# The hydra blocks' way in and way out: tokens halved by GpSimd and turned by DMAs, epsilon on GpSimd, orders listed anew

## What is computed

```python
x = L0_attn_hidden_states                                        # (4, 512, 512)
x = _layernorm(x + _L0_attn_ref(x, Wq, Wk, Wv, Wo), axis=-1)     # 32 heads of 16, causal, grouped keys
x = _layernorm(x + _L0_ffn_ref(x, gate, up, down), axis=-1)      # 4 bit weights, inner width 1376
x = _layernorm(x + _L1_attn_ref(x, ...), axis=-1)                # the hydra part
x = _layernorm(x + _L1_ffn_ref(x, gate, up, down), axis=-1)      # 4 bit weights, inner width 1792

def _L1_attn_ref(x, ...):
    h = transpose(x @ w_down.T + b_down, (1, 0, 2))   # 512 -> 128, "the way in"
    xmid = gelu(h)
    h = _hydra(_hydra(xmid))                          # two passes of convolution, scan, gate and norm
    h = xmid + alpha * xmid + (1.0 - alpha) * h
    h = h @ w_up.T + b_up                             # 128 -> 512, "the way out"
    return x + transpose(h, (1, 0, 2))
```

## Time and profile before

| | |
|---|---|
| median of 3 runs | 1409.86 us (1408.0 to 1412.52) |
| profiled execution | 1409.34 us, its span 1407.5 us |
| PE busy | 1330.7 us, 95% of the span |
| DVE busy | 1030.7 us, 73% |
| ACT busy | 795.1 us, 56% |
| POOL busy | 766.2 us, 54% |
| granted TensorE clock, mean | 0.981 of full |

### The profile page before, as it was taken

How to read it: one execution, slowest core, us unless ns; L and a number is a source line. 1 busy time by engine, 2 the same in 40 slices (tenths; PEclk the granted TensorE clock), 3 DMA queues, 4 the chain that set the end, 5 groups by cost and what they waited for, 6 DMA issues and landing times. The chain is left out here.

```text
span 1407.5 us, 32864 instructions
## 1 busy us (share of the span) xinstructions
PE 1330.7 (95%) x11934; PEld 978.2 (69%) x11934; DVE 1030.7 (73%) x2328; ACT 795.1 (56%) x1753; POOL 766.2 (54%) x963
## 2 busy tenths in 40 slices
PE   5788999989999999999999899999999999999998
PEld 2445866677678777868686667667777768586775
DVE  6988887876778889877777787968696778665121
ACT  3877787877687868877885244333424432331221
POOL 3656688688787577887544435254434434351221
PEclk8879999999999999999999999999999999999999
DMA  7573578578985554787662100641001000000000
GB/s 207 160 177 83 124 136 165 134 136 154 166 162 131 119 127 113 146 179 140 137 129 48 46 1 16 256 135 38 8 9 38 16 1 34 20 9 16 1 16 16
DMA packets 232356, 131.95 MB, mean 94 GB/s; under 512 B 151738, under 2 KB 215458, under 8 KB 231298
## 3 DMA queue, kind: packets, MB, share of 16 engines
q1 hardware_dynamic: 230956, 129.77, 39.9%
q10 hardware_dynamic: 1238, 0.07, 0.1%
HBM read 75.00 MB, written 19.92 MB: 67 GB/s over the span
## 5 line engine op out<-in xcount | busy, mean ns | idle before, releaser
L2004 PE MATMUL ps<-x3h,w1gu 128*128 128x256 f16 x1792 | 298.9, 273 | 3.4 <-DVE prod L1657 3.4
L1255 ACT ACTIVATE Pe<-ps,nmax 128x256 f32<-128x256 f32 (+3 forms) x512 | 252.8, 535 | 62.2 <-DVE nmax L1398 36.2
L1398 DVE TENSOR_REDUCE nmax<-ps 128x1 f32<-128x384 f32 (+3 forms) x352 | 222.7, 635 | 42.3 <-PE ps L1894 37.9
L2004 PE MATMUL ps<-x3l,w1gu 128*128 128x256 f16 x896 | 244.2, 273 | 0.0
L2004 PEld LDWEIGHTS ps<-x3h,w1gu 128*128 128x128 f16 x1792 | 175.3, 98 | 28.1 <-DVE prod L1657 5.0
L1393 DVE TENSOR_TENSOR pt<-ps,pt 128x512 f16<-128x512 f32 (+1 forms) x256 | 161.3, 632 | 34.8 <-ACT pt L1239 33.8
L1135 POOL TENSOR_TENSOR int1l<-prod,int1h 128x256 f16<-128x256 f32 x112 | 95.5, 858 | 137.1 <-ACT int1h L1354 137.1
L1239 ACT ACTIVATE pt<-ps 128x512 f16<-128x512 f32 (+1 forms) x256 | 143.3, 560 | 39.4 <-PE ps L1901 30.4
L1891 PE MATMUL ps<-kT,qT 128*128 128x256 f16 (+3 forms) x512 | 138.2, 305 | 16.0 <-ACT Pe L1255 15.0
L1901 PE MATMUL ps<-identf,Pe 128*128 128x128 f32 x928 | 148.0, 279 | 2.9 <-DVE pt L1393 2.0
L838 POOL TENSOR_TENSOR stp<-Pe,stp 128x512 f16<-128x512 f32 (+1 forms) x96 | 103.9, 1082 | 40.6 <-ACT stp L1247 40.5
(11 more groups left out here) (269 smaller groups left out, 3377.6 us busy)
## 6 DMA issues: line engine op xcount, KB each, us to landing
w1gu<-w_gu SPq DMA_DIRECT2D x7, 1024.0 KB, 8.1
x_dram<-xr SPq DMA_DIRECT2D x18, 256.0 KB, 3.1
xr<-in_x SPq DMA_DIRECT2D x16, 256.0 KB, 3.5
x2a<-x_dram SPq DMA_DIRECT2D x4, 1024.0 KB, 5.7
vq<-in_q1g SPq DMA_DIRECT2D x28, 128.0 KB, 2.5
vz<-in_z1g SPq DMA_DIRECT2D x28, 128.0 KB, 3.9
vs<-in_s1g SPq DMA_DIRECT2D x28, 128.0 KB, 4.6
w_gu<-vh SPq DMA_DIRECT2D x56, 64.0 KB, 2.3
```

The source lines that it names most:

```text
L1255: ins = act.activation(Pe[:, u % 2, x * w:(x + 1) * w], ps[:, u % 2, x * w:(x + 1) * w], ACT.Exp, bias=nmax[:, u % 4, x:x + 1])
L1398: dve.tensor_reduce(nmax[:, u % 4, 0:g], ps[:, u % 2, 0:g * w].rearrange("p (g w) -> p g w", g=g), AX, ALU.max, negate=True).then_inc(sem( ...
L2004: ins = pe.matmul(ps[:, bank, piece * H2:piece * H2 + H2], w1gu[:, j // 2, 2 * piece + pw, k, cols], px[:, k, h * H2:h * H2 + H2], start=( ...
```

## The change

The way in and the way out lose their transposes on TensorE. GpSimd splits each token tile into halves (`cs` in, `x3s` out: a copy to float16 and a subtraction), which it writes over tokens that are no longer needed, and one transposing DMA of 128 x 1024 float16 for each tile (`cd`, `x3d`) brings both halves turned to where TensorE reads them. w_down is split into halves as well (in `consts_a`), so that `c1_dn` becomes twelve float16 products. Steps `c1_tr`, `c1_te`, `x3tr`, `x3h` and `x3l` are gone. In all four layer norms epsilon is added by GpSimd ahead of its power instead of by VectorE. `x3s` waits until the next block's way in has been read (it writes into x2a), and x2a of block s waits for `x3d` of block s-2. The listing gets new durations and new parameters, and tiles 3 and 6 leave `LO_POOL`, so that VectorE makes their low halves. The core of the diff:

```diff
-LO_POOL = (3, 6, 7, 12, 13, 14, 15)
+LO_POOL = (7, 12, 13, 14, 15)
...
-        A("SP", "x2a", s, 3600, stored + ([("c1_tr", (s - 1, l)) for l in range(NB)] if s else staged(NT - 1)), R0)
+        A("SP", "x2a", s, 3600, stored + ([("c1_dn", (s - 1, l)) for l in range(NB)] + ([("x3d", (s - 2, l)) for l in range(NB)] if s > 1 else []) if s else staged(NT - 1)), R0)
...
-            A("PE", "c1_tr", (s, l), 440, after, R0, takes=0 if s else 1)
-            A("ACT", "c1_te", (s, l), 620, [("c1_tr", (s, l)), ("c1_dn", (s, l - 2)) if l >= 2 else None], R0, frees=None if s else ("c1_tr", (s, l)))
-            A("PE", "c1_dn", (s, l), 900, [("c1_te", (s, l)), ("weights_a", 0), ("h_raw", 2 * s - 1) if s else None], R0, takes=0 if s or l else 1)
+            A("POOL", "cs", (s, l), 1900, [("x2a", s), ("consts_a", 0), ("mix", s - 2) if s > 1 else None], R0)
+            A("SP", "cd", (s, l), 2100, [("cs", (s, l)), ("c1_dn", (s, l - 2)) if l >= 2 else ("c1_dn", (s - 1, l + 2)) if s else None], R0)
+            A("PE", "c1_dn", (s, l), 690, [("cd", (s, l)), ("h_raw", 2 * s - 1) if s else None], R0, takes=0 if s or l else 1)
...
-            A("PE", "x3tr", (s, l), 440, [("x3", (s, l)), ("x3l", (s, l - 3)) if l >= 3 else ("x3_sum", (s, 3 if l == 0 else l))], R0)
-            A("ACT", "x3h", (s, l), 600, [("x3tr", (s, l)), ("f1_gu", (s - 1, l // 2, NJ1 - 1), 1) if s else None], R0)
-            A("DVE", "x3l", (s, l), 690, [("x3h", (s, l))], R0)
+            A("POOL", "x3s", (s, l), 1900, [("x3", (s, l)), ("c1_dn", (min(s + 1, NI - 1), NB - 1))], RX)
+            A("SP", "x3d", (s, l), 2100, [("x3s", (s, l)), ("f1_gu", (s - 1, l // 2, NJ1 - 1), 1) if s else None], RO)
...
-WO_AT = 0
-CH0_AT = [-10 + 0.5 * c for c in range(NC0)]
-CH1_AT = [CH0_AT[-1] + 6 + 4 * c for c in range(NC1)]
-IN_AT = [-20, -10] + [FIRST[t] - 24 for t in range(2, NT)]
-FFN0_AT = [(37, 162), (226, 520), (402, 467), (482, 717), (721, 889), (877, 907), (899, 904), (912, 982)]
+WO_AT = 4
+CH0_AT = [-9 + 0.5 * c for c in range(NC0)]
+CH1_AT = [CH0_AT[-1] + 6 + 3 * c for c in range(NC1)]
+IN_AT = [-20, -10, -15, 50, 115, 75, 91, 138, 173, 151, 176, 184, 191, 220, 282, 308]
+FFN0_AT = [(74, 154), (154, 619), (460, 482), (566, 698), (694, 1051), (990, 1055), (946, 1475), (1294, 1366)]
...
+        def halves_of(s, l):
+
+            return (x2a[:, l - 1, :] if l else xmid[:, s % 2, :]).bitcast(F16)
...
+                if kind == "cd":
+                    s, l = key
+                    sp.wait_ge(sem("cs"), NB * s + l + 1)
+                    if s or l >= 2:
+                        sp.wait_ge(sem("c1_dn"), NB * s + l - 1)
+                    sp.dma_start_transpose(out=xTb[:, l % 2, :, :], in_=halves_of(s, l)).then_inc(sem(f"ld_cd{l % 2}"), 16)
+                if kind == "x3d":
+                    s, l = key
+                    sp.wait_ge(sem("x3s"), NB * s + l + 1)
+                    if s:
+                        sp.wait_ge(sem("f1_gu"), gate1(s - 1, l // 2, NJ1 - 1) + 1)
+                    sp.dma_start_transpose(out=x3hl[:, :, :, l * P:(l + 1) * P].rearrange("p a k n -> p (a k) n"), in_=x2a[:, l, :].bitcast(F16)).then_inc(sem(f"ld_x3d{l // 2}"), 16)
...
+                if kind == "x3s":
+                    s, l = key
+                    to = x2a[:, l, :].bitcast(F16)
+                    pool.wait_ge(sem("x3"), NB * s + l + 1)
+                    pool.wait_ge(sem("c1_dn"), NB * min(s + 2, NI))
+                    if s == NI - 1:
+                        pool.wait_ge(sem(f"ld_x3d{l // 2}"), 32 * s)
+                    own.link(pool.tensor_copy(to[:, 0:D], x3[s % 2][:, l, :]))
+                    pool.tensor_tensor(to[:, D:2 * D], x3[s % 2][:, l, :], to[:, 0:D], ALU.subtract).then_inc(sem("x3s"), 1)
+                if kind == "cs":
+                    s, l = key
+                    to = halves_of(s, l)
...
+                    own.link(pool.tensor_copy(to[:, 0:D], x2a[:, l, :]))
+                    pool.tensor_tensor(to[:, D:2 * D], x2a[:, l, :], to[:, 0:D], ALU.subtract).then_inc(sem("cs"), 1)
...
-                    pool.tensor_tensor(rstdc[:, l:l + 1], vec[:, l:l + 1], neghalf[:, 0:1], ALU.pow).then_inc(sem("rstd3"), 1)
+                    own.link(pool.tensor_scalar(rstdc[:, l:l + 1], mvc[:, l, 1:2], 1.0, EPS, ALU.mult, ALU.add))
+                    pool.tensor_tensor(rstdc[:, l:l + 1], rstdc[:, l:l + 1], neghalf[:, 0:1], ALU.pow).then_inc(sem("rstd3"), 1)
...
-            own.link(dve.bn_aggr(m, st[:, :]))
-            dve.tensor_scalar(v, m[:, 1:2], EPS, None, ALU.add).then_inc(ready, 1)
+            dve.bn_aggr(m, st[:, :]).then_inc(ready, 1)
...
-                    ins = pe.matmul(ps[:, dn_bank(s), l * P:(l + 1) * P], wdT[:, k, :], xTb[:, l % 2, k, :], start=(k == 0), stop=(k == KD - 1))
+                    for at, (px, pw) in enumerate(((0, 0), (0, 1), (1, 0))):
+                        ins = pe.matmul(ps[:, dn_bank(s), l * P:(l + 1) * P], wd[pw][:, k, :], xTb[:, l % 2, px * KD + k, :],
+                                        start=(k == 0 and at == 0), stop=(k == KD - 1 and at == 2))
```

More of the change, by code:

```diff
@@ L383, in way_out @@
         A("DVE", "x1_sum", t, 690, [e], r, frees=("wo", t))
-        A("DVE", "bn1", t, 1300, [("x1_sum", t), ("x1", t - 2) if t >= 2 else None], r)
-        A("POOL", "rstd1", t, 600, [("bn1", t)], r - 4)
+        A("DVE", "bn1", t, 1050, [("x1_sum", t), ("x1", t - 2) if t >= 2 else None], r)
+        A("POOL", "rstd1", t, 850, [("bn1", t)], r - 4)
         A("DVE", "x1", t, 570, [("rstd1", t)], r - 4)
@@ L452, in hydra @@
             A("DVE", "ul", q, 690, [("uh", q)], R5)
-            A("PE", "in", q, 3200, [("ul", q), ("h_u", q - 1) if q and p == 0 else None, ("x3l", (s - 2, 3)) if s > 1 and p == 0 else None], R5)
+            A("PE", "in", q, 3200, [("ul", q), ("h_u", q - 1) if q and p == 0 else None, ("x3_sum", (s - 2, 3)) if s > 1 and p == 0 else None], R5)
             A("ACT", "h_raw", q, 1400, [("in", q)], R5)
@@ L476, in hydra @@
             A("DVE", "h_yn", q, 1950, [("h_rs", q), ("consts_c", 0)], R5)
-            A("PE", "ytr", q, 900, [("h_yn", q)] + ([("x3_sum", (s - 1, 3)), ("x3l", (s - 1, 3))] if s and p == 0 else []), R5)
+            A("PE", "ytr", q, 900, [("h_yn", q)] + ([("x3_sum", (s - 1, 3))] if s and p == 0 else []), R5)
             A("ACT", "h_yT", q, 1050, [("ytr", q)], R5)
@@ L508, in ffn1 @@
                     old = ("f1_down", 4 * f + 2 * h - 1, 0) if j >= 2 and (f or h) else None
-                    e = A("PE", "f1_gu", (f, h, j), 1310, [e, old, ("x3l", (f, 2 * h + 1)), ("w1_load", j // 2) if f == 0 else None], mm, piece,
+                    e = A("PE", "f1_gu", (f, h, j), 1310, [e, old, ("x3d", (f, 2 * h + 1)), ("w1_load", j // 2) if f == 0 else None], mm, piece,
                           takes=1 if piece == 0 else 0)
@@ L760, in build @@
         mvd = cb("mvd", [P, 2, 2])
-        ved = cb("ved", [P, 2])
         rstdd = cb("rstdd", [P, 2])
         x3_odd = cb("x3_odd", [P, NB, D])
-        cb("ring_0_1", [P, 1328])
-        x3h = cb("x3h", [P, KD, S], F16)
-        x3l = cb("x3l", [P, KD, S], F16)
+        cb("ring_0_1", [P, 1320])
+        x3hl = cb("x3hl", [P, 2, KD, S], F16)
+        x3h, x3l = (x3hl[:, a, :, :] for a in (0, 1))
         cb("ring_6_7", [P, 1176])
@@ L1066, in pool_job @@
             if kind in ("rstd1", "rstd2"):
[L1067 removed]
+                v, r = (mv, rstd) if kind == "rstd1" else (mvb, rstdb)
                 o = key % 2
                 pool.wait_ge(sem("ve1" if kind == "rstd1" else "ve2"), key + 1)
[L1070 removed]
+                own.link(pool.tensor_scalar(r[:, o:o + 1], v[:, o, 1:2], 1.0, EPS, ALU.mult, ALU.add))
+                pool.tensor_tensor(r[:, o:o + 1], r[:, o:o + 1], neghalf[:, 0:1], ALU.pow).then_inc(sem(kind), 1)
             if kind == "x2_sum":
@@ L1506, in dve_constants @@
                 own.link(dve.tensor_scalar(A8[:, :], A8[:, :], 80.0, None, ALU.min))
+                own.link(dve.tensor_scalar(wd[0][:, :, :].rearrange("p k n -> p (k n)"), wd_load, WA_SCALE, 0.0, ALU.mult, ALU.add))
+                own.link(dve.scalar_tensor_tensor(out=wd[1][:, :, :].rearrange("p k n -> p (k n)"), in0=wd_load, scalar=WA_SCALE,
+                                                  in1=wd[0][:, :, :].rearrange("p k n -> p (k n)"), op0=ALU.mult, op1=ALU.subtract))
                 own.link(dve.tensor_scalar(inw[0][:, :], inw_load, WA_SCALE, 0.0, ALU.mult, ALU.add))
@@ L1691, in dve_stream @@
                     dve_hydra(dve, own, kind, key)
-                if kind in ("mix", "x3_sum", "bn3", "x3", "x3l"):
+                if kind in ("mix", "x3_sum", "bn3", "x3"):
                     dve_out(dve, own, kind, key)
```

123 lines of the change are left out of this document (46 added, 77 removed).

## The result

| | before | after |
|---|---|---|
| median of the runs, us | 1409.0 (1408.0 to 1412.5) | 1424.3 (1420.1 to 1426.7) |
| ratio, 95% interval | | 1.0101 [1.0082, 1.0121] |
| profiled execution, its span, us | 1409.3, 1407.5 | 1424.1, 1422.0 |
| PE busy, us | 1330.7 | 1314.8 |
| PE idle (span less busy), us | 76.8 | 107.2 |

The account below looks back on a forecast made before the run. TensorE was taken as the bound, busy 95% of the span; 1409.3 us less 17.7 of TensorE work plus 2.3 of waiting, with listing and attention at 0, gave 1394 us (this case 1389 to 1400, overall range 1380 to 1409).

Parts of the forecast that it names:

- the sum's rule: Behind the attention, what is taken off TensorE comes off the time if nothing else is late: 17.7 us.
- the new listing set at 0: Whole kernel's order: taken as 0; could win at most 19.5 us of attention idle and some of 10.9, or lose 15.
- the price that GpSimd's work has for VectorE: Hydra blocks: GpSimd busy 16 us more a block; net shortening 3.4 us over blocks 0 to 2, a third of VectorE's saving.
- PE's work: Way in and out: 10.7 us and 7.0 us less on TensorE, 17.7 together; PE busy about 1313 us.
- The rival in which float16 products bring nothing: Way in: float16 products at 0.11 us gain nothing, 7.0 us remain, 1402 us; chance 0.04.
- Turning: Each tile in and out: GpSimd 2.0 us plus a DMA landing in 4.0 us, 6.0 us, between 4.7 and 9.5.
- The reserve before f1_gu: Way out: 3.2, 5.0, 7.6 and 13.7 us left after turning in blocks 0 to 3; PE's final wait 2.3 us.
- The hydra chain: Hydra passes: gets shorter, VectorE spared 3.4 us a block, 3.4 us net over blocks 0 to 2.
- One of my signs that the mechanism is wrong: Hydra part: VectorE's operations would get longer in sum by more than they lost.
- The rival in which it sets the pace: Hydra chain grows some 3 us a block net through GpSimd's load: 1406 us (1403 to 1411); chance 0.15.
- the cover: Attention: VectorE, busy 480 of 610 us, absorbs 15 us more from 32 low halves; cost 0, or 15 if cover is gone.
- SP's queue: Way out of block 1: x3d waits behind a norm4 store in SP's list, 1405 to 1429, middle 1417; chance 0.08.

Follow-up runs that it names:

- e7: Changed kernel, same work, but listed as if x3d took 1.4 us with no margin, against the kernel before: 1411.6 us, ratio 1.0005.
- e18: Changed kernel with only SP's order of e7: second to fourth tile out of block 0 ahead of weight loads; 1429.3 us, ratio 1.0116 to the kernel before.
- e1: Kernel before with the six listing parameters of the changed kernel, its work otherwise unaltered: 1414.7 us, ratio 1.003 to the kernel before.
- e5: Changed kernel with way in and way out both as before, keeping epsilon on GpSimd and the new listing parameters: 1419.6 us, ratio 1.0065 to the kernel before.
- e3: Changed kernel with its way out as before (x3 transposed on TensorE, halves by ScalarE and VectorE): 1417.6 us, ratio 1.006 to the kernel before.
- e4: Changed kernel with its way in as before (x2a transposes and float32 products on TensorE): 1429.7 us, ratio 1.0141 to the kernel before.
- e9: Changed kernel, same order, GpSimd's subtraction for the low half on the way in made twice: 1443.5 us, ratio 1.0221 to the kernel before.
- e13: Changed kernel, same order, four one-column GpSimd operations before each low-half subtraction on the way in: 1439.9 us, ratio 1.0200 to the kernel before.
- e15: Changed kernel with way out on TensorE as before and a listing searched anew for the shortest plan: 1409.8 us, ratio 0.9987 to the kernel before.
- e2: Changed kernel with the six old listing parameters, LO_POOL among them: 1456.1 us, ratio 1.0327 to the kernel before.
- e6: Changed kernel with VectorE's first two f1_prod of layer 1 moved ahead of prod1: 1426.0 us, ratio 1.0115 to the kernel before.

## Why the prediction was wrong

The step that failed is the sum's rule that what is taken off TensorE comes off the time so long as no turned tile is late, with the new listing set at 0. PE lost 15.9 us of work and gained 30.4 us of idle time; it waited for VectorE in a new order. With the lists made otherwise for the same work (e7) 13.5 us of that come back. The second step is the price that GpSimd's work has for VectorE: the sum has 6.7 us of it over three blocks (10.1 spared, 3.4 left), and it is 23 us over the part behind the first h_raw.

**PE's work: right.** 17.7 us less were forecast, PE busy at about 1313; it is 1314.8, 15.9 less; the lower clock (0.973 against 0.981) may be part of the rest. The twelve products of a tile start at 966.84, 966.90 and so on up to 967.46, 0.06 us apart. The rival in which float16 products bring nothing falls.

**Turning: right in its parts.** GpSimd's copy takes 0.61 and its subtraction 1.15 us, as bounded. A tile in lands 2.8 us after its issue (2.7 to 4.2), one out in 2.8 by the median, less than the 4.0 I took. What I had not seen is the 12.4 us of tile (0,1), issued between 1 MB weight loads, its issue alone holding SP 6.5 us. e18, in which it is issued sooner, won nothing. The Trainium skill's 1309 ns for a block (VectorE: DVE Perf Modes, The three transpose paths), by which eight would take 10.5 us by my estimate, was not borne out on a quiet queue.

**The reserve before f1_gu: where the rule failed.** I compared the end of x3 of the second tile with the start of f1_gu and took the gap, less turning, for what PE could run into. This gap did not shrink to nothing, it grew. Taken to the first silu, it is 19.8, 22.0, 24.6 and 33.1 us in the four blocks, where it was 12.5, 13.9, 16.4 and 22.5 before (in block 3 from 1276.2 to 1309.3 us, before from 1271.9 to 1294.4). PE never waited for a turned tile. It lost its time elsewhere, between these points, and I had assumed that every us taken off PE there comes off the end so long as no turned tile is late. That would hold if PE were never idle for another reason; the earlier trace rows showed 10.9 us of idle up to 905, and I read these as small mismatches instead of as a sign that there VectorE's list leads. The step at 783 us shows it: the operand came at the same time as before, and what PE had saved was added to its wait.

**The hydra chain and VectorE: of the other sign, and not small.** The chain is 458.6 us long against 455.7; I had counted 3.4 us shorter, a third of what VectorE is spared. One of my signs that the mechanism is wrong did come: VectorE's operations in the hydra part got longer by more than they lost. The groups of which both kernels and the experiments make the same number in the same shape (871 operations behind the first h_raw, number times mean of the profile's rows) take 386.0 us in sum before and 409.0 after, 23 us more, against 17 us of x3l and epsilon that went. The same sum is 385.1 in e1 and 392.8 in e5, without GpSimd's halves, 392.1 in e3, 399.0 in e4 and 402.4 in e7. That these are collisions with GpSimd's work, as in the earlier trace rows, is borne out by e9 and e13. In that row VectorE's slowed operation starts 0.02 us ahead of GpSimd's and ends behind it, so it shows a collision and not who holds the port. The rival in which it sets the pace gave 1406 for a right-looking reason, but e5, with a chain of 445.4 us and a ratio of 1.0065, speaks against it.

**The attention: the cover held, its size was off.** The 32 low halves took 27.8 us on VectorE, the upper end of my 19 to 28, and from 140 to 750 us it is busy 22 us more, where I had counted 15 net. PE's idle time there moved by only 2.1 us, and the first h_raw comes 2.0 us earlier.

**The listing, taken at 0: the term that was missing.** I kept both ends, 15 us of loss through VectorE in the attention and some gain, and looked for the listing's effect only there. It is the largest term that a run shows. With the same work the list is worth 13.5 us (e7 against after), 0.7% (e15 against e3), and with LO_POOL's choice of engine in it 2.2% (e2 against after). Its loss in the changed kernel lies behind the attention: f1_prod behind prod1 (12.7 us of idle in that stretch where there were 3.4, and 3 us of clock, by e7), and perhaps the first two holes (14.4 us where there were 5.8). That this pair is due to the listing is not shown: every kernel that keeps the changed one's lists up to there has it to 0.1 us except e9 and e13, which hold GpSimd up, e7 at a ratio of 1.0005 among them; e1 has 5.8 and 1.6 there, e5 4.5 and 4.7, and no run repaired it alone. The plan that the listing makes was there to be read: it ended 1.7 us earlier than before, and I counted 15.

**SP's queue.** The wait for a norm4 ahead of an x3d was not there; the price I gave it (1417) came near the result for another reason.

What stays open: e7 gives back what the kernel lost against before, not the 15 us of the forecast; that these went to the first two holes and to VectorE's longer operations is argued from the counts, no run shows it. e7's gain was not divided between VectorE's list and those of PE, ScalarE and GpSimd, which change with it; only SP's was taken out. And the 6 to 11 us that the way out costs in e3 to e5 can't be split into its work and the list it comes with.

## What to carry to other kernels

When a kernel's order is made by a planner, a change of work is also a change of order, and the second can be the larger: compare the two orders step by step on each engine, above all what now stands behind long steps of an in-order engine, before counting what was saved, and read at what time the planner's own plan ends. Doubling a suspected cost shows what more of it would cost, not what the present amount costs; take it away as well, with the lists held still, and look at the engine that takes it over. And the longest hole need not be worth its length: moving two steps took 3.0 us of idle out of that stretch, and its work took 2.7 us longer.

## What the runs showed of the hardware

- Two DMA transposes of eight 128 x 128 blocks each, issued on SP behind loads of 1 and 1.8 MB, landed after 12.4 and 12.5 us where 2.8 is the median, and their issue held SP for 6.5 and 8.8 us where 1.23 is usual (kernel after).
- A delay of GpSimd of 1.1 us per tile by operations on one column (ratio 1.0200, e13) and one of the same length by a subtraction of 512 columns (1.0221, e9) can't be told apart by their intervals; but the second made the same 1043 instructions of VectorE 9.0 us longer, the first did not.
- The granted clock stayed at 0.95 in the stretch with two short holes as in that with one long one, and was 1.00 over the same stretch in e7, where the same 970 records took 127.7 instead of 130.9 and 133.6 us. In e6 it was 0.66 in the 5 us behind a hole of 1.99 us (923.4 to 928.4 us).
